# One addition of both parts of a step to the running sums, and a stage order drawn from newer lengths

## What is computed

```
x = x + 0.5 * ffn(layernorm(x))
x = x + attention(layernorm(x))
x = x + 0.5 * ffn(layernorm(x))
```

```
phi = k_val[..., None] * theta                     # K x H x M columns for each row
num_re = cumsum(p_w * cos(phi)); num_im = cumsum(p_w * sin(phi))     # along the rows
out_re = sum over m of (state_re * q_re + state_im * q_im)
out_im = sum over m of (state_im * q_re - state_re * q_im)
```

## Time and profile before

| | us |
|---|---|
| timed runs, median of 3 (lowest, highest) | 1239.68 (1239.1, 1245.08) |
| the profiled execution | 1235.89 |
| span of its trace | 1234.6 |
| PE busy | 970.2 (79%) |
| DVE busy | 719.1 (58%) |
| ACT busy | 586.2 (47%) |
| POOL busy | 441.7 (36%) |

### The profile page before, as it was taken

One profiled execution on the slowest core, in us unless ns is written; L12 is line 12 of the kernel. 1 busy time (PEld: TensorE's weight loads), 2 busy tenths in 40 slices (PEclk: granted clock), 3 DMA queues, 4 the chain that ended last, 5 costly groups with the idle time before them and its releaser, 6 DMA issues.

```text
span 1234.6 us, 10515 instructions
## 1 busy us (share of the span) xinstructions
PE 970.2 (79%) x3168; PEld 525.8 (43%) x3168; DVE 719.1 (58%) x1162; ACT 586.2 (47%) x1008; POOL 441.7 (36%) x424
## 2 busy tenths in 40 slices
PE   5899999944979888967935376798987897679993
PEld 2446664412435454523412133355454443336661
DVE  3400001277988998886898878799987961200000
ACT  4424444324536687656333254367668841314441
POOL 4154553003633363252000235427263301165552
PEclk9999999975989899987977777999998999799997
DMA  8965666336436776874233672348567553125666
GB/s 286 378 240 104 118 111 108 75 86 153 107 105 140 164 162 133 183 169 114 83 104 71 169 188 69 94 136 182 104 163 174 101 135 60 45 62 110 111 111 102
DMA packets 65227, 164.05 MB, mean 133 GB/s; under 512 B 11314, under 2 KB 11314, under 8 KB 63062
## 3 DMA queue, kind: packets, MB, share of 16 engines
q0 software_dynamic: 29440, 65.10, 30.0%
q1 hardware_dynamic: 35734, 98.30, 26.3%
HBM read 108.13 MB, written 63.60 MB: 139 GB/s over the span
## 4 chain that ended last, share of the span: by engine, by line
PE 46%; DVE 15%; DMA 12%; ACT 12%; POOL 7%; issue 7%; SPq 1%; POOLq 0%; DVEq 0%; ACTq 0%
PE yps L845 10%; PE hps L829 9%; PE hps L776 7%; PE yps L788 6%; PE misc L907 6%; POOL slots L1578 4%; DVE run L1395 2%; DMA outT<-tail_sb 2%; DMA x_rows<-tail_sb 2%; PE misc L873 2%; DMA x_rows<-ys,rows_i 2%; ACT xin L1045 2%; DVE trig L1402 1%; DMA q_cols<-xin 1%; PE misc L864 1%
## 5 line engine op out<-in xcount | busy, mean ns | idle before, releaser
L845 PE MATMUL yps<-w_all,hidden_sb 128*128 x368 | 180.8, 614 | 32.7 <-ACT hidden_sb L1010 32.7
L829 PE MATMUL hps<-w_all,hidden_sb 128*128 x736 | 176.5, 383 | 4.2 <-ACT hidden_sb L993 4.2
L829 PEld LDWEIGHTS hps<-w_all,hidden_sb 128*128 128x128 f32 x736 | 138.7, 192 | 52.6 <-issue 38.0
L1395 DVE TENSOR_TENSOR_SCAN run<-pwx,trig 128x512 f32<-128x512 f32 x128 | 149.3, 1207 | 19.0 <-ACT trig L1095 18.5
L1590 POOL DMA_INDIRECT xs<-x_normal,rows_i x92 | 107.5, 1168 | 137.2 <-PE xps L820 105.3
L776 PE MATMUL hps<-xnT,sw_sb 128*128 128x512 f32 x256 | 122.3, 627 | 4.8 <-ACT xnT L961 2.7
L788 PE MATMUL yps<-sw_sb,hidden_sb 128*128 128x512 f32 x256 | 120.4, 614 | 0.0
L1614 POOL DMA_INDIRECT x_rows<-ys,rows_i x48 | 82.4, 1717 | 72.3 <-ACT ys L1023 67.4
L845 PEld LDWEIGHTS yps<-w_all,hidden_sb 128*128 128x128 f32 x368 | 67.7, 194 | 95.1 <-issue 93.0
L1023 ACT ACTIVATE ys<-yps,slots 128x512 f32<-128x512 f32 x92 | 63.3, 688 | 88.4 <-PE yps L845 83.1
L1578 POOL DMA_INDIRECT slots<-told,dest_i x64 | 76.9, 1201 | 58.5 <-DVE cmp_a L1264 30.0
(11 more groups left out here) (201 smaller groups left out, 1592.4 us busy)
## 6 DMA issues: line engine op xcount, KB each, us to landing
qx<-q_cols SPq DMA_DIRECT2D x128, 256.0 KB
x_normal<-xin SPq DMA_DIRECT2D x32, 256.0 KB, 5.3
w_all<-in_w_experts SPq DMA_DIRECT2D x8, 1024.0 KB, 8.0
xin<-x_rows SPq DMA_DIRECT2D x32, 256.0 KB, 5.0
turns_sb<-in_w_out SPq DMA_DIRECT2D x3, 1536.0 KB, 9.9
xin<-in_x SPq DMA_DIRECT2D x16, 256.0 KB, 4.4
sum_rows<-ys SPq DMA_DIRECT2D x16, 256.0 KB, 3.0
xin<-sum_rows POOLq DMA_DIRECT2D x16, 256.0 KB, 8.9
```

The costliest lines, as they stand in the source:

```text
L829: t = PE.matmul(hps[:, bank, 0:H], xT[:, j % 2, c, :], w_all[:, bass.ds(expert[j] + c * H, H)], start=c == 0, stop=c == KC - 1)
L845: t = PE.matmul(yps[:, bank, :], hb[:, j % 2, ec, :], w_all[:, bass.ds(expert[j] + (KC * H + ec * D), D)], start=ec == 0, stop=ec == EC - 1)
L1395: t = VE.tensor_tensor_scan(run[:, c, :], pwx[:, n // M, :], trig[:, n % 2, c, :], 0.0, ALU.mult, ALU.add)
```

## The change

There are two parts.

In a step, the imaginary part is now made first, in the second half of the `qx` buffer (or of `outT` for `m = 0`), and the real part after it, in the first half of the same buffer, which the subtraction has just read. Both lie side by side then, and `sum_parts` is one addition of 1,024 columns. The signals follow: one `out_summed` for a step, and `added` in the order imaginary, real. `phases` waits for the real addition of the step two before; `load_query` waits for the one sum.

Some lengths in the planner are others.

```diff
-            piece("POOL", ("w_rest",), 13.0, ("POOL", ("load", 0)))
+            piece("POOL", ("w_rest",), 9.0, ("POOL", ("load", 0)))
...
-            piece("POOL", ("load", q), 4.6, ("DVE", ("load", q)))
-            piece("ACT", ("norm", q), 2.4, ("POOL", ("load", q)))
-            piece("SP", ("norm", q), 1.8, ("ACT", ("norm", q)))
+            piece("POOL", ("load", q), 3.6, ("DVE", ("load", q)))
+            piece("ACT", ("norm", q), 3.0, ("POOL", ("load", q)))
+            piece("SP", ("norm", q), 2.4, ("ACT", ("norm", q), -2.1))
...
-                piece("PE", s, 0.7, ("ACT", ("norm", q)), *turned_rows, bank=[("xps", ("ACT", s))])
+                piece("PE", s, 0.7, ("ACT", ("norm", q), -0.7 * (TB - 1 - tb)), *turned_rows, bank=[("xps", ("ACT", s))])
...
-                piece("PE", s, 3.7, *kept_rows, *start[:1], *blocks_end, bank=[("hps", ("ACT", s))])
+                piece("PE", s, 3.6, *kept_rows, *start[:1], *blocks_end, bank=[("hps", ("ACT", s))])
...
-                piece("PE", s, 0.7 if j % AT_ONCE else 1.9, ("POOL", ("bring", g, j), 3.3),
+                piece("PE", s, 0.6 if j % AT_ONCE else 1.3, ("POOL", ("bring", g, j), 3.3),
...
-            piece("DVE", ("c_sum", b, n), 2.8 if m else 1.4, ("DVE", ("c_times", b, n)),
+            piece("DVE", ("c_sum", b, n), 2.6 if m else 1.4, ("DVE", ("c_times", b, n)),
...
             def add_parts(b, n):
+
                 half, m = divmod(n, M)
                 re2, im2 = trig[:, n % 2, :, :], qx[:, n % NQX, :, :]
-                re = outT[:, half, 0, :] if m == 0 else re2[:, 0, :]
-                im = outT[:, half, 1, :] if m == 0 else im2[:, 0, :]
+                re, im = [outT[:, half, i, :] if m == 0 else im2[:, i, :] for i in range(2)]
                 if m == 0 and b > 0:
                     vec.wait_ge(*y_made.at((b - 1, half * VH + VH - 1)))
-                vec.wait_ge(*real_made.at((b, n)))
-                VE.tensor_tensor(re, re2[:, 0, :], re2[:, 1, :], ALU.add).then_inc(*added.of((b, n, 0)))
                 vec.wait_ge(*imag_made.at((b, n)))
                 VE.tensor_tensor(im, im2[:, 0, :], im2[:, 1, :], ALU.subtract).then_inc(*added.of((b, n, 1)))
+                vec.wait_ge(*real_made.at((b, n)))
+                vec.wait_ge(*added.at((b, n, 1)))
+                VE.tensor_tensor(re, re2[:, 0, :], re2[:, 1, :], ALU.add).then_inc(*added.of((b, n, 0)))
 
             def sum_parts(b, n):
                 half = n // M
-                re, im = outT[:, half, 0, :], outT[:, half, 1, :]
                 vec.wait_ge(*added.at((b, n, 0)))
-                VE.tensor_tensor(re, re, trig[:, n % 2, 0, :], ALU.add).then_inc(*out_summed.of((b, n, 0)))
-                vec.wait_ge(*added.at((b, n, 1)))
-                VE.tensor_tensor(im, im, qx[:, n % NQX, 0, :], ALU.add).then_inc(*out_summed.of((b, n, 1)))
+                VE.tensor_tensor(outT[:, half, :, :], outT[:, half, :, :], qx[:, n % NQX, :, :],
+                                 ALU.add).then_inc(*out_summed.of((b, n)))
```

More of the change, by code:

```diff
@@ L368, in plan_blocks @@
                 s = ("one", g, j)
-                piece("PE", s, 1.9, ("ACT", ("x", g, j)),
+                piece("PE", s, 1.8, ("ACT", ("x", g, j)),
                       *([("SP", ("w_expert", E - 1), 10.0)] if g == 0 else []), bank=[("hps", ("ACT", ("mid", g, j)))])
@@ L375, in plan_blocks @@
                 s = ("two", g, j)
-                piece("PE", s, 1.9, ("ACT", ("mid", g, j)), bank=[("yps", ("ACT", s))])
+                piece("PE", s, 1.8, ("ACT", ("mid", g, j)), bank=[("yps", ("ACT", s))])
                 piece("ACT", s, 0.7, ("PE", s),
@@ L401, in plan_head @@
             piece("DVE", ("a_stats", b), 3.4, *[("POOL", ("a_add", b, tb), 3.8 - 0.8 * (TB - 1 - tb)) for tb in range(TB)])
-            piece("POOL", ("a_stats", b), 4.6, ("DVE", ("a_stats", b)))
-            piece("ACT", ("a_norm", b), 2.4, ("POOL", ("a_stats", b)))
+            piece("POOL", ("a_stats", b), 3.6, ("DVE", ("a_stats", b)))
+            piece("ACT", ("a_norm", b), 3.0, ("POOL", ("a_stats", b)))
             for tb in range(TB):
                 s = ("a_turn", b, tb)
-                piece("PE", s, 0.7, ("ACT", ("a_norm", b)), *turned_rows, bank=[("misc", ("ACT", s))])
+                piece("PE", s, 0.7, ("ACT", ("a_norm", b), -0.7 * (TB - 1 - tb)), *turned_rows, bank=[("misc", ("ACT", s))])
                 piece("ACT", s, 0.6, ("PE", s))
@@ L623, in macaron @@
         imag_made = signal("s_imag", BN)
-        added = signal("s_added", [(b, n, i) for b, n in BN for i in range(2)])
-        out_summed = signal("s_out_summed", [(b, n, i) for b, n in BN if n % M for i in range(2)])
+        added = signal("s_added", [(b, n, i) for b, n in BN for i in (1, 0)])
+        out_summed = signal("s_out_summed", [s for s in BN if s[1] % M])
         out_scaled = signal("s_out_scaled", BHALF)
@@ L1379, in phases @@
                     last = (b, n - 2) if n >= 2 else (b - 1, STEPS + n - 2)
-                    vec.wait_ge(*(out_summed if last[1] % M else added).at((*last, 0)))
+                    vec.wait_ge(*added.at((*last, 0)))
                 vec.wait_ge(*convolved.at((b, half, CW - 1)))
@@ L1432, in scale_output @@
                 vec.wait_ge(*spread_den.at((b, half)))
-                vec.wait_ge(*out_summed.at((b, half * M + M - 1, 1)))
+                vec.wait_ge(*out_summed.at((b, half * M + M - 1)))
                 if half:
@@ L1782, in load_query @@
                 if n >= NQX:
-                    sp.wait_ge(*(out_summed if (n - NQX) % M else added).at((b, n - NQX, 1)))
+                    sp.wait_ge(*(out_summed.at((b, n - NQX)) if (n - NQX) % M else added.at((b, n - NQX, 0))))
                 elif b > 0:
-                    sp.wait_ge(*out_summed.at((b - 1, STEPS + n - NQX, 1)))
+                    sp.wait_ge(*out_summed.at((b - 1, STEPS + n - NQX)))
                 for g in range(QH):
```

## The result

The changed kernel takes 1251.32 us in the median of 15 runs (1244.86 to 1256.79), the kernel before 1239.1 us in the same comparison (1231.91 to 1248.78). The ratio is 1.0089, with a 95% interval of 1.0065 to 1.0113: slower by 11.0 us (8.1 to 14.0). The profiled execution has a span of 1246.8 us, against 1234.6.

A forecast was written before the change was run, and what follows sets the result against it. No engine was taken to bound the whole program; DVE's attention steps bound three full stretches. Sums +5.0 us on the path, buffers 0 and order 0, added to the 1239.68 us median, gave 1244.7 us; range 1231 to 1257 us.

The forecast's parts named there:

- rival 3: Order gets worse: turns planned 2.5 us too early block PE in half of 12 places, +7; 1251.9 us; chance 0.20.
- The price of a wait on the neighbour: DVE's sums: a wait on the instruction directly in front costs 0.115 us, three a step; period 8.09 becomes 8.37 us.
- DVE's busy time and instructions: DVE over the whole program: 56 instructions fewer (1106), busy time up by about 10 us from 719.1.
- What of it is on the path: Of +14.2 us of DVE time, only the 18 running sums in the three full stretches count: 18 x 0.275 = +5.0 us.
- rival 2: DVE's added time counts nearly everywhere, since its idle time is not slack: all 14.2 us, 1253.9 us; chance 0.15.
- the count of running sums in the full stretches: 596 to 668, 784 to 853 and 384 to 492 us, where DVE is nearly always busy: 18 sums at +0.275 us each.
- The order, "at 0, as the two kinds of error pull apart": The planner's order from the new lengths: taken at 0, some lengths nearer the chip, POOL's further away; bounds -14 and +15.
- The sign that the prediction named to tell rival 2 from rival 3: If the time rises by over 10 us: DVE idle before the scans or PE idle before L741 tells them apart.
- The argument that no order shortens the latency of the loads: Said against a better order gaining from DVE's 41.8 us idle, 668 to 1008 us: it is behind loads and norms.
- The bound of +15: Upper bound on the new order's cost: half of 12 x 2.5 us, PE waiting at turns planned too early.
- The buffers at 0: Trig tile and qx: releases at other times gain or cost nothing; bounds 0 and +0.3 us once.
- rival 4: Waits on the neighbour cost nothing in DVE's sums, only the saving of 1.3 us on the path: 1238.4 us; chance 0.05.

The follow-up runs named there:

- e1_sums_only: The kernel before with the new sums alone, all planner lengths and the stage order as before; 1.0033 (1.0009 to 1.0057) to the kernel before, +4.1 us.
- e4_waits_alone: The kernel before with its four additions, each of the last three made to wait for the one directly in front; 1.0014 to the kernel before, +1.7 us.
- e2_order_only: The kernel before with the planner's new lengths alone, its four additions kept; 1.0088 (1.0055 to 1.0121) to the kernel before, +10.9 us.
- e10_interleaved: e8_before_moved with the next step's first phase operation issued between a step's two scans; 1.0296 to the kernel before, slower by 37 us.
- e8_before_moved: The kernel before with group 2's slot reading on DVE and first row turn on PE and ACT moved later; 0.9978 to the kernel before, -2.7 us.
- e14_gap_back: e10_interleaved with the imaginary subtraction made to wait also for the real addition in front; 0.995 to the kernel before, 1237.66 us.

## Why the prediction was right, and where it was not

*The direction and the range* held: slower was forecast at 0.4%, with 1231 to 1257 us; it is 0.9%, 1251.32 us. The number itself was 6.6 us too low, and outside the forecast's own range of 1240 to 1250: the full range held because it took in the rivals, and the result lies at rival 3's 1251.9. So the forecast's account, sums alone and an order at 0, was right in its direction and in its smaller part.

*The price of a wait on the neighbour* held. L1418 and L1426 start 0.03 us behind the end of their neighbours, while the successors of the four additions before start 0.07 to 0.09 ahead of it. One term was missing: the second wait in front of the real addition, 0.07 us. That makes the period 8.46 instead of 8.37, and 64 x 0.07 = 4.5 us of DVE time on top of the 14.2.

*DVE's busy time and instructions*: +10.2 us and 1106, as forecast.

*What of it is on the path*: +5.0 forecast, +4.1 measured with the sums alone (1.1 to 7.1), and rival 2 (all of it, 14.2) is refuted by `e1_sums_only` and `e4_waits_alone`. That the count of running sums in the full stretches is the right rule is not shown, and its good number may be luck. The same count gives `e4_waits_alone` 18 x 0.44 = 7.9 us, and it measured 1.7, at most 4.8. And in the traces, one execution each, `e1_sums_only` falls behind the kernel before by 1.0 us from step (0, 8) to (1, 4), where the count has 2.5, and by 2.8 us from there to (1, 12), between 497 and 600 us, where it has nothing.

*The order, "at 0, as the two kinds of error pull apart"*: this step failed. It costs +10.9 us alone. The sign and size are near rival 3. The sign that the prediction named to tell rival 2 from rival 3 points there too: DVE's idle time before the scans fell from 19.0 to 11.3 us, and PE's before L741 rose from 88.0 to 101.4. But it is one turn that waits some 13 us longer, not six of twelve that wait 2.5, and what it costs was not tested by itself. What was tested is another stage that waits for a DMA, one whose length the change did not touch. The argument that no order shortens the latency of the loads behind which DVE is idle overlooked that an order decides what else stands behind such a wait. The bound of +15 held.

*The buffers at 0*: held for the sums; in `e1_sums_only` the idle time before the real products (L1402) is 0.2 us in all, as before. In the changed kernel it is 1.9 us, over the bound of 0.3, in two waits for query loads; this came with the order, since `e2_order_only` has 1.5.

*The rule that waits cost nothing* (rival 4; the Trainium skill, "VectorE: DVE Perf Modes", "The DRAIN you can't avoid"): `e4_waits_alone` shows the additional 0.12 us a wait directly, with the same four operations. But in the time of the whole kernel 0.44 us a step are only +1.7 us, and in `e10_interleaved` one wait fewer a step costs 37 us, since another engine is held up (last section).

## What to carry to other kernels

Fusing two operations saves only what one start costs (0.07 us here), and pays for every wait that now falls on the instruction directly in front (0.12 us each, 0.07 for a second one); keep one independent instruction between writer and reader. If an order is drawn from lengths, look at what stands behind each stage that waits, on every engine together, since two such waits in a row hide one another; and compare orders by their times, since a length nearer to the chip did not always give a faster one. Before you take the last pause out of a step on VectorE, look at what GpSimd does beside it and who waits for that: here it cost 3%.

## What the runs showed of the hardware

A chain of VectorE operations, nearly all with two inputs in SBUF, without a pause between them can hold up a GpSimd indirect DMA, once for 20 us here. One scatter took 20.72 us instead of 0.96. It does not do so each time: three that began at 322.47, 323.94 and 325.24 us, the last two in the same chain, took 1.16, 1.00 and 0.96. What decides which is held, and what frees one in the midst of a chain, is not shown. The mean of the 64 scatters was 1.48 us in `e10_interleaved`, 1.24 in `e8_before_moved`, 1.19 in `e14_gap_back`, and 1.17 and 1.15 in `e1_sums_only` and `e4_waits_alone`, whose full steps have four pauses instead of one. With a pause of 0.03 to 0.10 us in each step, no scatter took over 6.7 us in any of the thirteen other kernels. This also offers a reason why the added waits of `e4_waits_alone` cost so little; that was argued and not shown.

The Trainium skill, page "SBUF — State Buffer", section "Who interferes with whom", says that a VectorE instruction with two inputs in SBUF contends with a GpSimd instruction that reads SBUF, that the ports they share are an exclusive lock, and, where it speaks of VectorE's 2-port modes, that whoever issues first has them for the whole instruction while the other is blocked. The traces agree that GpSimd's instruction is held up, and show more: it can stay so over a chain of instructions, in one case for 20 us.
